# Expert and second latent weights streamed in pairs: two rows of 128 columns per transfer, in a ring with slots twice as large

## The reference

```
x = x + layernorm(attention(layernorm(x)))
x = x + layernorm(ffn(layernorm(x)))
attention: q, k, v = x @ Wqkv + b (4096 -> 3 x 1024), one head,
           softmax(q k' / 32) v, then @ Wo (1024 -> 4096) + bo
ffn:  routing = sum of the top 2 of x @ gate_w (8 experts)
      shared  = relu(x @ up_w)**2 @ down_w       (4096 -> 8192 -> 4096)
      latent  = x @ fc1_w                        (4096 -> 2048)
      routed  = ((latent @ expert_w) * routing) @ fc2_w (2048 -> 2048 -> 4096)
      layernorm(shared + routed) * gamma + beta
```

## Time and profile before

| | |
|---|---|
| median of three timed runs | 5543.91 us |
| fastest and slowest of the three | 5366.46 and 5588.54 us |
| profiled execution, its time | 5271.11 us |
| its span, slowest core (core 2) | 5269.3 us |
| spans of the eight cores | 5229.4 to 5269.3 us |
| granted TensorE clock, mean of the cores | 0.858 to 0.868 |

### The profile page before, as it was taken

How to read it: one execution, slowest core, us unless ns; L and a number is a source line. 1 busy time by engine, 2 the same in 40 slices (tenths; PEclk the granted TensorE clock), 3 DMA queues, 4 the chain that set the end, 5 groups by cost and what they waited for, 6 DMA issues and landing times. The chain is left out here.

```text
span 5269.3 us, 45340 instructions; the slowest of 8 cores (5229.4 to 5269.3 us)
## 1 busy us (share of the span) xinstructions
PE 3600.2 (68%) x18500; PEld 1658.5 (31%) x18500; DVE 854.3 (16%) x958; ACT 284.5 (5%) x447; POOL 291.7 (6%) x539
## 2 busy tenths in 40 slices
PE   3676876763560566777765877771198999899961
PEld 1252643521220222333322333320043444344420
DVE  2002112104314100000000000017200000100035
ACT  0000000210110000000000000002000000000010
POOL 0000000000010000000000000000000000100000
PEclk8888988886785798999987888985599999999975
DMA  5984342244126688999977999962434443334313
GB/s 90 197 186 112 113 129 79 67 81 127 47 66 151 127 195 185 213 208 208 215 176 163 208 212 214 211 145 87 97 120 137 153 152 130 134 142 156 148 48 128
DMA packets 172841, 758.14 MB, mean 144 GB/s; under 512 B 17879, under 2 KB 42584, under 8 KB 104030
## 3 DMA queue, kind: packets, MB, share of 16 engines
q0 software_dynamic: 98800, 478.25, 43.5%
q1 hardware_dynamic: 73838, 276.99, 14.2%
HBM read 746.85 MB, written 243.28 MB: 188 GB/s over the span
## 5 line engine op out<-in xcount | busy, mean ns | idle before, releaser
L239 PE MATMUL psp<-C2f,wrf 128*128 128x512 bf16 x5120 | 1164.0, 390 | 224.8 <-DMA wrf<-Wup 126.7
L239 PEld LDWEIGHTS psp<-C2f,wrf 128*128 128x128 bf16 x5120 | 507.6, 100 | 883.3 <-issue 324.1
L239 PE MATMUL psp<-C1f,wdf 128*128 128x512 bf16 x2048 | 512.5, 414 | 172.6 <-DMA wdf<-Wdn 123.7
L239 PE MATMUL psp<-C2a,wr2a 128*128 128x512 bf16 x1536 | 357.7, 397 | 177.2 <-PEq L223 106.1
L239 PE MATMUL psp<-Ab,wdf 128*128 128x512 bf16 x2048 | 457.5, 382 | 0.0
L239 PEld LDWEIGHTS psp<-C1f,wdf 128*128 128x128 bf16 x2048 | 212.8, 105 | 467.1 <-issue 276.7
L239 PE MATMUL psp<-moeb,wxf 128*128 128x512 bf16 x1024 | 255.8, 411 | 85.9 <-DMA wxf<-Wf 51.6
L332 PE MATMUL psp<-C1f,onb 128*128 128x512 bf16 x128 | 37.9, 469 | 356.8 <-PEq L223 356.8
L239 PEld LDWEIGHTS psp<-Ab,wdf 128*128 128x128 bf16 x2048 | 201.5, 98 | 245.5 <-issue 16.3
L239 PEld LDWEIGHTS psp<-C2a,wr2a 128*128 128x128 bf16 x1536 | 154.8, 102 | 379.4 <-issue 216.0
L239 PE MATMUL psp<-wr2a,C2a 128*128 128x128 bf16 x4096 | 234.7, 221 | 17.0 <-DMA wr2a<-Wqkv 17.0
(11 more groups left out here) (89 smaller groups left out, 1654.3 us busy)
## 6 DMA issues: line engine op xcount, KB each, us to landing
wrf<-Wup POOLq DMA_DIRECT2D x64, 1024.0 KB, 14.7
up_scr<-wrf SPq DMA_DIRECT2D x64, 1024.0 KB, 13.9
wdf<-Wdn POOLq DMA_DIRECT2D x64, 1024.0 KB, 16.8
dn_scr<-wdf SPq DMA_DIRECT2D x64, 1024.0 KB, 13.4
wrf<-up_scr POOLq DMA_DIRECT2D x64, 1024.0 KB, 6.1
wdf<-dn_scr POOLq DMA_DIRECT2D x64, 1024.0 KB, 6.9
wr2a<-qkv_scr POOLq DMA_DIRECT2D x56, 1024.0 KB, 6.0
wr2a<-Wqkv POOLq DMA_DIRECT2D x24, 1024.0 KB, 16.7
```

Source lines behind the costliest of these rows:

```text
L239: return self._push(self.t.matmul(*a, **k))
```

## The change

Four things are done.

1. The ring wxf keeps its two slots, but a slot holds two rows (1 MB in bf16). Each load of Wex, ex_scr, Wf2 and f2_scr takes two rows at once, and so does each store to ex_scr and f2_scr. The groups of matmuls stay as they are: the even one reads the first half of a slot and the odd one the second. A group waits for the load of its pair, and a slot is free when the odd group of its pair is done.
2. xf32 and yf32 of the attention are released with it. For the end of the FFN new buffers xf32f and yf32f are allocated in each tile where wdf has just been released. That frees the room that the larger ring takes.
3. At the end of each tile there is one more block, in which SyncE waits for the last loads and stores of these buffers.
4. A semaphore sgc is declared and not used; default arguments of four functions are taken away, which alters no instruction.

```
-    xf32 = sbt(p2_es, "xf32", [128, 2, EW, T], F32, side="right")
-    yf32 = sbt(p2_es, "yf32", [128, 2, EW, T], F32, side="right")
+    xf32 = sbt(att_es, "xf32", [128, 2, EW, T], F32, side="right")
+    yf32 = sbt(att_es, "yf32", [128, 2, EW, T], F32, side="right")
...
-    wxf = sbt(ffn_es, "wxf", [128, 2, 16, 128], BF16, side="right")
+    wxf = sbt(ffn_es, "wxf", [128, 2, 2, 16, 128], BF16, side="right")
...
-        exsrcs = [Wex[mc] for mc in range(16)] if ot == 0 else \
-                 [ex_scr[mc] for mc in range(16)]
+        def _pair(dram, p):
+            return dram[2 * p:2 * p + 2].transpose([1, 0, 2, 3])
+        exsrcs = [_pair(Wex, p) for p in range(8)] if ot == 0 else \
+                 [_pair(ex_scr, p) for p in range(8)]
...
-            scr=([ex_scr[mc] for mc in range(16)] if ot == 0 else None))
+            scr=([_pair(ex_scr, p) for p in range(8)] if ot == 0 else None))
...
-                sl = (i_x0 + mc) % 2
+                sl = (i_x0 + mc // 2) % 2
                 for lc in range(16):
-                    t.matmul(psp[:, bk], wxf[:, sl, lc], latb[:, lc],
+                    t.matmul(psp[:, bk], wxf[:, sl, mc % 2, lc], latb[:, lc],
...
-                           "waits": [rX.wait(i_x0 + mc)], "nmm": 16,
+                           "waits": [rX.wait(i_x0 + mc // 2)], "nmm": 16,
...
-        exlgv[:] = [t_base0 + b + 1 for b in range(16)]
-        exlgv2[:] = [stm.n + 15 * (b + 1) for b in range(16)]
+        exlgv[:] = [t_base0 + 2 * p + 2 for p in range(8)]
+        exlgv2[:] = [stm.n + 15 * (2 * p + 2) for p in range(8)]
...
         dn_es.close()
+        ep_es = contextlib.ExitStack()
+        xf32 = sbt(ep_es, f"xf32f{ot}", [128, 2, EW, T], F32, side="right")
+        yf32 = sbt(ep_es, f"yf32f{ot}", [128, 2, EW, T], F32, side="right")
...
         block(sync=fsync, vector=fvec)
+        block(sync=lambda s: (s.wait_ge(sxs[0].h, sxs[0].n),
+                              s.wait_ge(sxs[1].h, sxs[1].n),
+                              s.wait_ge(sxl[0].h, sxl[0].n),
+                              s.wait_ge(sxl[1].h, sxl[1].n)))
+        ep_es.close()
```

More of the change, by code:

```diff
@@ L153, in build_program @@
     stm = Sem(es, nc, "stm")
+    sgc = Sem(es, nc, "sgc")
     sv = Sem(es, nc, "sv")
@@ L708, in build_program, with ysync @@
         r2b = r_rep[:].unsqueeze(1).broadcast_to([128, EW, T])
-        def ysync(s, ot=ot, tq0=tq0, sv0=sv0):
+        def ysync(s, ot=ot, tq0=tq0):
             for k in range(NCH // EW):
@@ L720, in ysync, with yvec @@
                     yf32[:, k % 2]), 16)
-        def yvec(v, sv0=sv0, cl0=cl0, cs0=cs0):
+        def yvec(v):
             for k in range(NCH // EW):
@@ L957, in build_program @@
         i_x1 = rX.nload
-        f2srcs = [Wf2[oc] for oc in range(NCH)] if ot == 0 else \
-                 [f2_scr[oc] for oc in range(NCH)]
+        f2srcs = [_pair(Wf2, p) for p in range(16)] if ot == 0 else \
+                 [_pair(f2_scr, p) for p in range(16)]
         f2lgv, f2lgv2 = [], []
@@ L963, in build_program @@
             rX, "rX", f2srcs, f2lgv, f2lgv2,
-            scr=([f2_scr[oc] for oc in range(NCH)] if ot == 0 else None))
+            scr=([_pair(f2_scr, p) for p in range(16)] if ot == 0 else None))
         block(gpsimd=pre_f2)
@@ L971, in mk @@
             def mk(t, oc=oc, bk=bk):
-                sl = (i_x1 + oc) % 2
+                sl = (i_x1 + oc // 2) % 2
                 for lc in range(16):
-                    t.matmul(psp[:, bk], wxf[:, sl, lc], moeb[:, lc],
+                    t.matmul(psp[:, bk], wxf[:, sl, oc % 2, lc], moeb[:, lc],
                              start=(lc == 0), stop=(lc == 15))
@@ L979, in build_program @@
             groups.append({"mms": mk, "evac": [("v", ev, None)],
-                           "waits": [rX.wait(i_x1 + oc)], "nmm": 16,
+                           "waits": [rX.wait(i_x1 + oc // 2)], "nmm": 16,
                            "bank": ("c", 6)})
         t_base0 = st_.n
-        f2lgv[:] = [t_base0 + b + 1 for b in range(NCH)]
-        f2lgv2[:] = [stm.n + 15 * (b + 1) for b in range(NCH)]
+        f2lgv[:] = [t_base0 + 2 * p + 2 for p in range(16)]
+        f2lgv2[:] = [stm.n + 15 * (2 * p + 2) for p in range(16)]
         mm_stream(groups, gpsimd_fn=rest_f2, sync_fn=sync_f2wb)
@@ L1044, in build_program, with t4v @@
         r4b = r_rep[:].unsqueeze(1).broadcast_to([128, EW, T])
-        def t4v(v, ss0=ss0):
+        def t4v(v):
             for k in range(NCH // EW):
@@ L1052, in t4v, with t4s @@
                 sv.inc(v.tensor_mul(yf32[:, k % 2], yf32[:, k % 2], r4b))
-        def t4s(s, sv0=sv0):
+        def t4s(s):
             for k in range(NCH // EW):
@@ L1072, in build_program, with fsync @@
         r5b = r_rep[:].unsqueeze(1).broadcast_to([128, EW, T])
-        def fsync(s, ot=ot, tq0=tq0, sv0=sv0):
+        def fsync(s, ot=ot, tq0=tq0):
             for k in range(NCH // EW):
@@ L1085, in fsync, with fvec @@
                     yf32[:, k % 2]), 16)
-        def fvec(v, cl0=cl0, cs0=cs0):
+        def fvec(v):
             for k in range(NCH // EW):
```

## The result

Over eleven timed runs of each kernel the median fell from 5512.47 to 5439.23 us, and the ratio of the kernel after to the kernel before is 0.9894, with a 95% interval of 0.9855 to 0.9934. So the kernel is faster by a little over 1%, clear of no change and short of 2%. The forecast was a factor of 0.9908 and a time of 5493 us, in a range of 5280 to 5576. The factor is the better test of the two: the median of the kernel before itself moved, from the 5543.91 us that the forecast was put on to 5512.47.

What follows compares the result with a forecast made beforehand. It took transfers to bound the first tile and a single transfer's delay the second: -26.8 - 23.1 + 1.6 = -48.3 us on 5271.1, factor 0.9908. On the 5543.91 us median that gives 5493 us, range 5280 to 5576.

Steps and rivals of the forecast that it cites:

- The first tile's cycle: First tile's expert and fc2 stages: one turn of the two pair slots takes 21.3 us, between 18.2 and 24.3.
- the idle part: First tile's cycle: 3.0 us with DMA engines idle, paid once a cycle whatever its size.
- The start: First load to first matmul of a wxf stage: 15.0 us in the first tile, 8.3 in the second.
- the last two pairs: End of the first tile's expert and fc2 stages: TensorE's work after the last two loads, 15.8 us.
- Theory A: From the experiments: the gain is a transfer's fixed cost, paid half as often.
- The Trainium skill's rule: Each transfer costs about 2.0 us plus bytes at 436 GB/s; first tile's cycle 20.3 us, gain 36.8 us.
- The second tile: Expert and fc2 stages there: no wait for loads, 6.9 us a pair, 23.1 us gained.
- The layout and the block: Moved xf32 and yf32 cost nothing; the waiting block at each tile's end adds 0.8 us, twice, 1.6 us.
- The test that was set too tight: Any stage outside the four moving over 5 us at equal granted clock would show that the layout matters.
- One tile only: Rival: first tile's cycle doubles to 24.3 us, only the second tile gains, -18.2 us in all; chance 0.20.
- the DMA engines fill up: Rival: first tile's cycle falls to 18.2 us, -79.3 us in all; chance 0.18.
- The slower chain: Rival: a slot's own load and store make the first tile's cycle 29.2 us, +30.8 us in all; chance 0.08.

Runs made afterwards that it cites:

- e3: Changed kernel with four one-row slots, one transfer per row, still waited for and released in pairs; 5181.6 us.
- e4: Changed kernel with stores in single rows, loads still in pairs; first tile's expert and fc2 stages 92.7 and 175.7 us.
- e2: Changed kernel with four one-row slots, each released by itself when its own matmuls and store are done; 5166.3 us.
- e6: Changed kernel with three slots of a pair in place of two; 5208.5 us.
- e1: Kernel before with only xf32 and yf32 moved and the tile-end block added, wxf as it was; 5236.4 us beside 5245.3 before.
- e5: Kernel before, unaltered, profiled a second time; first tile's up stage 638.6 us, down stage with what follows 926.1 us.
- e9: Same kernel as e2, timed beside the kernel before; 5203.8 and 5227.4 us, ratio of means 0.986, no interval.

## Why the prediction came out right, point by point

**The first tile's cycle: form right, size off by 1 us.** The prediction took 18.2 us of transfer work and 3.0 us of idle time, 21.3 us; measured are 20.35 us in the after profile. Windows over just these cycles give a DMA share of 0.76 before and 0.87 after: 9.2 us of work and 2.9 idle in 12.16 us, then 17.7 and 2.6 in 20.35. So the idle part did stay about as it was while the work nearly doubled, and each of the two terms came out some 0.4 to 0.5 us below its forecast. The start was taken as 15.0 us and measured 15.0, the last two pairs 15.8 and 15.7. In fc2 seven cycles, each 0.95 us shorter than forecast, make 6.7 us, and that is the whole distance between the gain measured, 27.4 us, and the 20.8 forecast. For expert the gain was 7.0 against 6.0 on the profiled cores, and 10.9 by the medians over the cores. What e3 and e4 add is that the number of transfers does not set the idle part: a cycle with the same bytes and twice the loads, or twice the stores, is as long. One reading of the prediction was also a little off: TensorE was busy 65% of the expert window, but 69% of that of fc2; nothing in the sum hangs on it.

**But not every reason given for it holds.** The prediction named issue, start and completion of a load and of a store as the idle part. Transfers issued behind one another in a batch do not add theirs (e3, e4). The idle time goes with how slots are handed over and how many there are. Hand them over one row at a time, with the same bytes and the same transfers as in e3, and the DMA share goes from 0.83 to 0.94 (e2); keep the pairs and add a third slot, and it is 0.94 as well (e6). Theory A, one of the two on record for the experiments, fell in three of them (e2, e3, e4).

One part of a cycle was not named at all. These are two stretches of TensorE in the fc2 stage of the first tile after:

```profile
2704.53 8.75 PE L240 MATMUL psp<-moeb,wxf 128*128 128x512 bf16 x32 [3.56 <-DMA wxf<-Wf]
2714.07 7.07 PE L240 MATMUL psp<-moeb,wxf 128*128 128x512 bf16 x32 [0.79 <-DVE C2f L981]
```

Behind an idle time of 3.56 us the granted clock was 0.64 for the first 3.5 us, for the most part the lower level of 1.2 GHz; behind 0.79 us it was 1.00. So a wait of some 3 us brings 1.7 us of slower matmuls with it, and pairs halve the number of waits. Whether those 1.7 us lie on the path of the first tile's cycle no run here separates.

**The start: the right number for a wrong reason.** The prediction had the loads of a batch land together and took 15.0 us as the middle of 1 MB and 3 MB; 15.0 was measured. But the loads land one behind the other, at 8.5 and 14.1 us, and TensorE waits for the last at the meeting. The middle came out because the last landing follows the bytes of the whole batch. The first load is in fact served first, and for that case the prediction named 9 us; it is the meeting, which the prediction left out here, that makes 15.0 of it. That was in part luck, and so it was with the 8.3 us of the second tile, where the loads landed 5.2 and 7.7 us after the first issue and TensorE began at 8.3.

**The Trainium skill's rule** ("DMA: Bandwidth & Descriptors", "Anatomy of one DMA — SWDGE (gpsimd) path", 2.0 us fixed a transfer) gave a cycle of 20.3 us by the prediction's estimate, and 20.35 was measured. The section speaks of transfers that GpSimd issues, while the stores, which make half of the 4.0 us saved, are issued by SyncE. And by e3 the agreement is a coincidence: with the two fixed costs a cycle put back, the cycle did not get longer, (2806.87 - 2667.72) / 7 = 19.9 us from the timeline of e3, of which the second row is below. For a load alone the estimate from its figures is 2.0 + 2.4 = 4.4 us for 1 MB, where 5.2 us were measured in the second tile.

```profile
2806.87 8.66 PE L239 MATMUL psp<-moeb,wxf 128*128 128x512 bf16 x32 [2.30 <-DMA wxf<-Wf]
```

**The second tile: right within 2 us a stage.** Forecast 23.1 us, measured 5.5 + 15.7 = 21.2. No wait is left. The landing, taken as 6.1 us from the up stage, was 5.2, so the margin under 6.90 us was wider than the 0.2 us that worried me. The start was forecast at 8.3 and measured 8.4 and 8.3. What is missing is in the matmuls: from the first to the last they took 57.96 and 112.9 us (the windows after less the starts) where 57.3 and 111.8 were forecast. On core 2 of the same profile they took 57.3 and 112.5 us, so most of what is missing is a difference between cores.

**The layout and the block.** Taken as 0 and 1.6 us; measured: nothing beyond scatter (e1, e5), and 0.04 us where the first tile ends (5.83 against 5.79).

**The test that was set too tight.** The prediction said that another stage moving by over 5 us would show the layout at work. Up moved by 5.9 and down by 7.0 us, and yet e2 and e9, one and the same kernel, differ by 5.0 and 18.2 us there. A threshold for a stage has to come from two profiles of the same kernel.

**The rivals.** "One tile only" (cycle 24.3 us) and "the DMA engines fill up" (18.2 us) both miss the measured 20.35. The slower chain (29.2 us) was far off: wxf loads landed after 10.9 us and stores after 6.4 us at the median, not 14.7 and 13.9. Two slots and not three were under way, and e6 bears that out: with three slots of the same size its loads of Wf2 landed after 14.8 us and the stores after 12.0. From the page after:

```profile
wxf<-Wf POOLq DMA_DIRECT2D x16, 1024.0 KB, 10.9
f_scr<-wxf SPq DMA_DIRECT2D x16, 1024.0 KB, 6.4
```

## What to carry to other kernels

When a ring of weight slots starves, ask for bytes under way and for how finely slots are handed back, before asking for larger transfers: with the same SBUF, four slots of one row beat two slots of a pair by 9 to 11 us in each stage bound by the transfers, and pairs moved row by row did as well as pairs. Then look at what a stage's first matmul really waits for. Here it was, by every trace, the last load of the first batch and not the one that it reads, because the batch ends in a meeting of all engines; that is why a larger ring made every start dearer. Issuing the batch behind the last load of the stage before wins the start back where the DMA engines have room (35 us in the second tile) and nothing where they are full. A cheaper remedy, a batch of one load ahead of the meeting and the others beside the stage, was not run. An estimate from the landings after (8.5 and 5.2 us, and 0.6 us behind them) is a start of 9.1 in place of 15.0 us in the first tile and of 5.8 in place of 8.3 us in the second. And take the cost of a cycle apart into what grows with the bytes and what is paid once a turn; that gave the size of the gain within 1 us a cycle here.

## What the runs showed that was not expected

- A start takes as long as the bytes of its batch, in whatever pieces: 15.0 us for two of 1 MB and 15.2 us for four of 0.5 MB in the first tile; three of 1 MB take 20.6 us at the median in e6. The first load is served first (it landed after 8.5 us and 6.8 us in the first two), but TensorE does not start with it.
- A load of 1 MB in two runs a partition landed after 5.2 us at the median in the second tile. The up stage's loads of the same size, in one run, had 6.1 us in the profile before and 5.2 us in the one after, so that the difference lies between executions or cores and not between the shapes. This is the page's row after:

```profile
wrf<-up_scr POOLq DMA_DIRECT2D x64, 1024.0 KB, 5.2
```
- GpSimd's issue of a pair takes 0.70 us, where a row took 0.53 us. No stage is seen to be longer for it: e3, with single rows, is as long as the change.
